# Causal mask moved from TensorE to VectorE, three-part maxima, dense keys and new turn orders in a four-layer decoder kernel

## Time and profile before

| | |
|---|---|
| median of the runs | 1035.74 us (1035.72 to 1036.4) |
| the profiled execution | 1035.02 us, span of its instructions 1033.0 us |
| TensorE matmul busy | 908.0 us, 88% of the span |
| VectorE busy | 540.3 us, 52% |
| ScalarE busy | 456.7 us, 44%, of it 106.5 in 83 table loads |
| GpSimd busy | 51.4 us, 5% |
| mean granted TensorE clock | 0.944 |

### The profile page before, as it was taken

One profiled execution on the slowest core, in us unless ns is written; L12 is line 12 of the kernel. 1 busy time (PEld: TensorE's weight loads), 2 busy tenths in 40 slices (PEclk: granted clock), 3 DMA queues, 4 the chain that ended last, 5 costly groups with the idle time before them and its releaser, 6 DMA issues. The chain is left out here.

```text
span 1033.0 us, 22562 instructions
## 1 busy us (share of the span) xinstructions
PE 908.0 (88%) x9368; PEld 701.5 (68%) x9368; DVE 540.3 (52%) x1569; ACT 456.7 (44%) x927; POOL 51.4 (5%) x71
## 2 busy tenths in 40 slices
PE   7698998999989988987887989989999889998952
PEld 5267975789778775765455757968888667785631
DVE  4823677443364664356654853755234647454335
ACT  2045364253465662572343234244445554445432
POOL 2300000000010000000000000001001000000000
PEclk9799999999999999998899999999999989999955
DMA  9100004010000210112000000040000300000000
GB/s 341 38 3 2 2 1 164 2 36 2 2 18 19 121 42 2 42 56 93 1 13 1 2 2 1 2 164 14 25 1 19 121 19 2 1 2 1 2 0 21
DMA packets 6838, 36.12 MB, mean 35 GB/s; under 512 B 721, under 2 KB 4305, under 8 KB 5458
## 3 DMA queue, kind: packets, MB, share of 16 engines
q1 hardware_dynamic: 6738, 34.68, 9.0%
HBM read 34.15 MB, written 0.52 MB: 34 GB/s over the span
## 5 line engine op out<-in xcount | busy, mean ns | idle before, releaser
L672 PE MATMUL bank<-xT,weights_F 128*128 128x256 f32 x832 | 200.0, 383 | 2.4 <-ACT p L1817 2.4
L672 PEld LDWEIGHTS bank<-xT,weights_F 128*128 128x128 f32 x832 | 151.0, 191 | 23.3 <-ACT p L1817 3.9
L680 PEld LDWEIGHTS bank<-weights_F,p 128*128 128x128 f32 x1088 | 134.1, 193 | 14.7 <-issue 6.0
L680 PE MATMUL bank<-weights_F,p 128*128 128x128 f32 x1088 | 141.6, 279 | 1.8 <-ACT p L1893 1.0
L1742 ACT ACTIVATE p<-bank 128x512 f32<-128x512 f32 x160 | 84.5, 605 | 110.5 <-PE bank L491 110.4
L1682 ACT ACT_TABLE_LOAD x83 | 106.5, 1283 | 17.5 <-PE bank L524 9.7
L1346 DVE SCALAR_TENSOR_TENSOR res<-bank,comb,res 128x128 f32<-128x128 f32 x184 | 55.8, 345 | 72.5 <-PE bank L680 69.8
L1817 ACT ACTIVATE p<-bank 128x512 f32<-128x512 f32 x72 | 42.4, 597 | 91.1 <-PE bank L672 90.7
L1183 DVE TENSOR_REDUCE m_wide<-bank 128x4 f32<-128x512 f32 x96 | 60.6, 682 | 37.9 <-PE bank L779 31.1
L1362 DVE TENSOR_TENSOR p<-p,bank 128x512 f32<-128x512 f32 x72 | 49.3, 685 | 56.3 <-ACT p L1817 34.7
L1893 ACT ACTIVATE p<-bank 128x512 f32<-128x512 f32 x64 | 36.6, 598 | 47.6 <-PE bank L672 47.3
(11 more groups left out here) (316 smaller groups left out, 1367.2 us busy)
## 6 DMA issues: line engine op xcount, KB each, us to landing
weights_F<-in_L1f SPq DMA_DIRECT2D x2, 4096.0 KB, 13.0
weights_F<-in_L0f SPq DMA_DIRECT2D x2, 3456.0 KB, 12.3
weights_F<-in_L2f SPq DMA_DIRECT2D x2, 3456.0 KB, 11.7
weights_Y<-in_L1x_kv SPq DMA_DIRECT2D x2, 1024.0 KB, 10.2
weights_Z<-in_L1x SPq DMA_DIRECT2D x2, 1024.0 KB, 11.1
weights_Y<-in_L2a SPq DMA_DIRECT2D x2, 898.0 KB, 4.5
weights_Z<-in_L2x SPq DMA_DIRECT2D x2, 449.0 KB, 3.4
weights_L3m<-in_L3m SPq DMA_DIRECT2D x2, 288.0 KB, 5.9
```

The source lines that it names most:

```text
L672: m = mm(b[:, k * NT:(k + 1) * NT], W[weight][:, f:f + P], s.xT[:], start=True, stop=True)
L680: m = mm(b[:, tk(u)], h[:, tk(u)], w, start=k == 0, stop=k == len(chunks) - 1)
```

## The change

1. **Transposed mask.** The bfloat16 mask matmuls of lines 509 and 983 go. VectorE takes, in the bank, the minimum of the transposed scores less maxima and the constant `upper_t` (-big above the diagonal, 3e38 else), one instruction of 128 x 512 per bank (`causal_only`), and ScalarE's `exps` waits for it (`causal`). This holds for the causal block of L0x and for L3a. The mask ahead of the maxima (lines 485, 775) and in L3x (1044) stays on TensorE.
2. **Three-part maxima.** `split_maxima` writes each maximum as a sum of three numbers that bfloat16 holds, side by side in `m_wide`: four VectorE instructions on 128 x 16, each waiting for the one before. `mT` becomes bfloat16, `pick_bf` has three ones per head, and `less_maximum` becomes a bfloat16 matmul.
3. **No block-diagonal keys.** `scores8` takes the block-diagonal queries as stationary operand and the plain keys as moving one, 16 matmuls of 128 columns in place of 4 of 512. `spread_heads` for `bd_c` and `bd_k` goes, in L0a, L0x and L2x; that for `bd_q` comes ahead of the scores. In L3x `bd_c` now comes from the context's `ctxT` and is made by GpSimd in L3a, with the scores in 16 matmuls likewise.
4. **Evened shapes.** In L1x the picks use 64-row tiles, as the scores they alternate with do.
5. **New orders** in `TURN_ORDER` for all five engines.

```diff
-                    if st == "L0x":
-                        pe.wait_ge(*told("maxima"))
-                    else:
-                        pe.wait_ge(*freed(st, "s", u, 0, 3))
+                    pe.wait_ge(*told("maxima"))
                     filled(tr(b[:, 0:T], s.m_wide[:, u], IDENT), st, "mT", u)
-                def scores8(st, u, keys, mask=None, blk=0):
+                def scores8(st, u, keysT, mask=None, blk=0):
...
-                    for i, b in enumerate(banks):
-                        filled(mm(heads(b[:], 4), s.qT[rows32(i), tk(u)], keys[rows32(i), u], start=mask is None, stop=True),
-                               st, "s", u, blk, i)
+                    for j in range(4):
+                        for i, b in enumerate(banks):
+                            m = mm(b[:, j * T:j * T + T], s.bd_q[rows32(i), u, j], keysT[rows32(i), tk(u)], start=mask is None,
+                                   stop=mask is None or j == 3)
...
                 def less_maximum(u, i, b, j, last):
-                    return mm(b[:, j * T:j * T + T], const("pick")[rows32(i), j:j + 1].to_broadcast([32, P]), s.mT[rows32(i), u],
+                    return mm(b[:, j * T:j * T + T], pick_bf[rows32(i), j:j + 1].to_broadcast([32, P]), s.mT[rows32(i), u],
                               start=False, stop=last)
...
-                def scores8_t(st, u, keysT, mask=None, blk=0):
+                def scores8_t(st, u, keysT, blk=0):
...
-                    if mask is not None:
-                        for b in banks:
-                            mm(heads(b[:], 4), ident_bf[:], among(mask, 4), start=False, stop=False)
                     less_maxima(st, u, banks, blk)
...
                             for n, b in enumerate(banks):
-                                m = less_maximum(u, n, b, j, True)
+                                r, at = n % 2, 4 * (n // 2) + j
+                                m = mm(b[:, j * T:j * T + T], pick_bf[rows64(r), 4 + at:5 + at].to_broadcast([64, P]),
+                                       s.mT[rows64(r), u], start=False, stop=True)
...
-                        for b in banks:
-                            mm(heads(b[:], 4), ident_bf[:], among(neg_causal_t_bf[:], 4), start=False, stop=False)
                         less_maxima("L3a", u, banks)
...
+                def split_maxima(u):
+                    part = lambda k: heads(s.m_wide[:, u], 4)[:, :, 4 * k:4 * k + 4]
+                    done = o.count(dve.tensor_copy(heads(s.m_part[:, 0], 4), part(0)))
+                    yield
+                    dve.wait_ge(*done)
+                    done = o.count(dve.tensor_tensor(part(1), part(0), heads(s.m_part[:, 0], 4), ALU.subtract))
+                    yield
+                    dve.wait_ge(*done)
+                    done = o.count(dve.tensor_copy(heads(s.m_part[:, 1], 4), part(1)))
+                    yield
+                    dve.wait_ge(*done)
+                    o.count(dve.tensor_tensor(part(2), part(1), heads(s.m_part[:, 1], 4), ALU.subtract), sem("maxima"))
...
+                def causal_only(st, u, blk=0):
+                    for i in range(4):
+                        if i:
+                            yield
+                        b = heads(bank(st, "t", u, blk, i)[:], 4)
+                        o.count(dve.tensor_tensor(b, b, among(const("upper_t"), 4), ALU.min), sem("causal"))
...
-                    spread_heads(s.bd_k, s.kT, sem("L0x_own_keys"))
+                    spread_heads(s.bd_q, s.qT, sem("queries"))
...
-                def exps(st, u, first, scale, blk=0):
+                def exps(st, u, first, scale, blk=0, masked=False):
...
+                        if masked:
+                            act.wait_ge(*told("causal"))
...
-                    act.wait_ge(*ring.freed((pair, "L3a", "xT")))
-                    for j in range(4):
-                        o.count(act.activation(s.bd_c[:, :, j], by_sample(s.xT[:]), ACT.Identity,
-                                               scale=const("head16in64")[:, j:j + 1]), sem("L3x_bd") if j == 3 else None)
...
                 def L3a():
+                    for u in range(NS):
+                        o.count(pool.tensor_tensor(s.bd_c[:, u], among(s.ctxT[:, tk(u)], 4), over(const("head16in64"), T), ALU.mult),
+                                sem("L3x_bd"))
+                    yield
                     yield from rest()
```

## The result

The changed kernel takes **1055.4 us** (median of 4 runs, 1053.05 to 1059.59) against 1036.07 for the kernel before, run beside it: ratio 1.0174, 95% interval 1.0117 to 1.0231. It is slower by about 18 us. I had forecast 998.6, a range of 978 to 1028, and 8% for slower. The profiled execution took 1059.59 us.

The account below looks back on a forecast made before the run. TensorE's own work was taken to set most of the time, chains between engines the rest. 1035.0 - 46.4 (TensorE) + 9.0 (VectorE) + 3.3 (loads) - 3.0 (tail) = 997.9, plus 0.7 for the median: 998.6 us, range 978 to 1028.

Parts of the forecast that it names:

- TensorE's cut: TensorE's work in L0x, L2x, L3a and L1x, from cheaper picks, dropped masks and even shapes: 46.4 us saved.
- the mask: Transposed-mask matmuls leaving TensorE in L0x (1.21 x 8) and L3a (0.97 x 8): 17.5 us saved.
- The pick group: 16 bfloat16 pick instructions on TensorE at 28 ns each: 0.44 us a group, where float32 took 0.89.
- L1x's evening: One tile shape for L1x's scores and picks: four rounds from 4.31 to 2.5 us, 14.5 us saved in all.
- VectorE's part: Splits (26.9 us) and minima (16) lengthen chains by 42.9 us; at 21% not covered by the other stream, 9.0 show.
- VectorE's steps show in full: Rival: VectorE's in-order queue holds up the other stream, so 42.9 us show for 9.0: 1032.5 us, chance 0.09.
- The clock: Rival: lower TensorE busy share drops attention stretches' granted clock from 0.92 to 0.84, costing 20 us: 1019, chance 0.11.
- My row for the lower level: The same 32 score instructions take 2.06 us at the clock's upper level and 3.35 at the lower.
- The keys: Scores in 128-column pieces without block-diagonal keys have as many columns as before, so they cost TensorE nothing.
- ScalarE's loads: 42 more table loads, 54 us, where a feed-forward meets a softmax; 3.3 us show, bounds 0 and 54.
- the tail: Stream a's second L3x unit moves into stream b's lonely last chain: 3 us less, between 0 and 6.
- ScalarE becomes the bound: Rival: each expert's SiLU waits for two table loads; if all 54 us show, 1049 us, chance 0.08.

Follow-up runs that it names:

- b1: Kernel before with bfloat16 picks of one part, no splits, L1x with 64-row picks, old orders: 1004.7 us, ratio 0.9705.
- m1: Kernel before with only the transposed causal mask moved to VectorE's minima, float32 picks, old orders: the minima cost 11 us.
- n1: Kernel before with the mask of the transposed scores left out, no minima added, exponentials at a hundredth scale: the mask's cost from here to before is 11.8 us.
- p1: Kernel before with only the three-part bfloat16 maxima and picks, splits and L1x's 64-row picks, old orders: ratio 0.9943.
- pm1: Kernel before with three-part picks and VectorE's minima together, block-diagonal keys kept, old orders: ratio 1.0128, 1046.7 us.
- o1: Changed kernel under the orders of before, new pieces put in: as slow as the changed kernel, +20 us (12 to 28) against before.
- o2: Kernel before under the orders of the change, its keys' pieces put back: 52 us slower than before, ratio 1.0505.
- m2: Kernel before with VectorE's minima added and TensorE's masks kept, old orders: the minima's chain costs 22.7 us against before.
- c1: Changed kernel with its picks back in float32, same splits, minima, keys and orders: 34 us more than the changed kernel (0.0329).

## Why the prediction was wrong

**TensorE's cut, 46.4 us: right.** Picks and L1x came to 30.5 (0.45 x 32 + 14.5 = 28.9 forecast), the mask to 11.8 (17.5): 42.3, and the work at the upper clock fell by 47. The pick group was mis-sized, 0.23 for 0.44, and L1x's evening came to 7.9 where 14.5 had 3.6 for its picks and 10.9 for the shapes. I had set aside my own lower bound, 0.24, for a spacing seen in two other kinds of instruction. There the Trainium skill (TensorE: Matmul & The Clock Gate, "Wait — 56ns, not 53.3ns?") served badly: starts never closer than about 25 ns. In b1 the four matmuls of a foursome start 7 ns apart and the foursomes every 56. Nor did the trace of before agree, as I had said: 28 ns is the average of a merged row, and within's picks single starts lie 5 to 8 ns apart in places too. The same page of the Trainium skill, Part 3 ("Packing small matmuls — row/col tiling"), says that tiles at different rows run beside each other, and the trace agrees with that, with these 7 ns.

**VectorE's part, 9.0 us: the step that failed.** I multiplied a chain of 42.9 us by TensorE's idle share, 21%. Measured by old orders: splits 24.6 and minima 23.3, 48 together, more than the whole chain. In the profiled executions TensorE's idle time alone grows by 12.8 and 17.5, 30 of the 42.9; the rest is mostly the lower clock, 8 and 3. Under the new orders the two cost 11.3 and 10.2. An idle share tells how often TensorE has nothing to do, not how often a delay is caught: the order of every engine is fixed, and where the next matmul in it waits, as at 77.56 us above, nothing behind it can be done first. That orders made for the new lengths halve the price agrees with this. My rival 'VectorE's steps show in full' was this, at 0.09. And I had named what is queued behind a waiting minimum without pricing it: 21.9 us of VectorE standing in m1.

**The clock, a rival at 0.11 and 20 us, and at nothing in the sum: some 40 us, its largest gap.** From 0.946 to 0.903, at 8.9 us for 0.01, is 38 us; that is a slope from one kernel laid on another, so an estimate. The split of the profiled executions gives 40: the work fell by 47 and TensorE's busy time by 6. These 40 are not to be added to the prices above, which were read from times and hold their share of the clock. Nor did it come as I had put it. b1 and n1 cut work and add no waits, and they keep 0.942 and 0.944; p1, pm1 and o1, with longer waits, fall to 0.931, 0.917 and 0.915, and o2 to 0.918 with no work cut at all. The sum of the waits doesn't set it either: m1 and m2 have 145 us of idle time and keep 0.940. What decides is open. My row for the lower level was misread besides: the stretch of the 3.35 us has a mean granted clock of 0.59, so its last instructions ran at the upper level.

**The keys, priced at nothing: wrong both ways**, 9.3 us lost by old orders (5 by the medians) and 8.0 gained by new ones, L3x's share included.

**ScalarE's loads 3.3, the tail -3.0: not separable.** They are part of the new orders, which cost the old code 52 us and gain the changed code 2 (o1 to after), less than the intervals can tell. The rival 'ScalarE becomes the bound' isn't borne out: in the changed kernel TensorE waits for SiLU's activations (L1846) for 0.9 us in all, and o1 has no more loads than before and is no faster.

**The sums nearly close in both frames.** Old orders: -30.5 picks -11.8 mask +24.6 splits +23.3 minima +9.3 keys = +14.9 us, measured +20 (12 to 28) for o1. New orders, from o2's 1.0505: -34.1 (c1) -13.8 -8.0 +11.3 +10.2 = -34.4 us, so 1.0173; measured 1.0174. That it closes to a tenth of a us is luck: each term is good to several us, and L1x's even shapes, 7.9 by old orders, were not measured here and are not in it. So the new orders halve what the steps cost and make use of the keys, some 50 us better for this code than for the old, and cost 52 in themselves. Of these 52, in the profiled executions, 18 are idle time and 34 the lower clock. What in them costs that is open. The traces offer a reading that I did not test: stream a's second L0a, small steps, runs in them from 511 to 535 us beside b's L3x (its matmuls from 507 to 541), where before it ran beside b's L3a, and the stretch from 480 to 580 has a clock of 0.71 for 0.95, 0.75 in o2.

## What to carry to other kernels

In a program whose engines follow fixed orders, count a microsecond added to a chain at its full price unless you can name the instruction that stands behind the wait and can go first; a busy or idle share is no discount, and orders laid out anew for the longer chain took off only half. Take TensorE's waits twice, once as idle time and once as the clock of what comes after. Moving work off the engine that is the bound onto one that it waits for cost twice here what it saved. Before paying for an exact offset, ask whether it divides out.

## What was not expected of the hardware

- Matmuls of 32 rows and 128 bfloat16 columns in four row tiles start 7 ns apart, a foursome every 56 ns. In float32 a foursome of instructions goes every 111 ns, and there are twice as many (32 in 0.89 us).
- The clock varies between runs of one program, 0.934 to 0.957, and the time by 2% with it.
- 23 us of useless matmuls in 20 us of TensorE's waits were free, and the mean clock rose by 0.013.
